# Mixer 0 and the dense experts: w1 loaded, bounded and split at the start of the mixer, and GpSimd's token halves made to wait for the normalised tiles

## What is computed

```python
# mixer of layer 0: a short convolution, linear attention with prefix sums, a gate, then dense experts
y = xp[:, 0:Tv]*w_dw[:,0] + xp[:, 1:Tv+1]*w_dw[:,1] + xp[:, 2:Tv+2]*w_dw[:,2]
x = x + einsum('btd,ed->bte', y, w_pw)
q, k, v = split(einsum('btd,ed->bte', x, w_qkv))      # 16 heads of 8, rotated
q_phi, k_phi = elu(q) + 1, elu(k) + 1
num   = einsum('bthd,bthdm->bthm', q_phi, cumsum(k_phi[..., :, None] * v[..., None, :]))
denom = sum(q_phi * cumsum(k_phi))
attn  = einsum('btd,ed->bte', num / (denom + 1e-6), w_o)
x = x + sigmoid(einsum('btd,ed->bte', x - x_before, w_gate) + b_gate) * attn
h = layernorm(x) * ln_g + ln_b
gw  = softmax(h @ w_moe_gate.T)                       # 4 experts, all used
hid = silu(einsum('btd,efd->btef', h, w1) + b1)       # w1: 4 experts x 512 x 128
s = x + einsum('bte,bted->btd', gw, einsum('btef,edf->bted', hid, w2) + b2)
# ffn of layer 0: 16 experts, top 1 with a capacity of 160 tokens, chosen from the layer's first norm
```

## Time and profile before

| what | us |
|---|---|
| runs shown | 1209.11, 1211.19, 1211.15 (median 1211.15) |
| the profiled execution | 1211.67 |
| its span, first to last instruction | 1209.9 |
| mean granted clock of TensorE | 0.987 of full speed |
| PE busy | 1143.2 (94%) |
| POOL busy | 839.1 (69%) |
| DVE busy | 825.1 (68%) |
| ACT busy | 686.0 (57%) |

### The profile page before, as it was taken

One profiled execution on the slowest core, in us unless ns is written; L12 is line 12 of the kernel. 1 busy time (PEld: TensorE's weight loads), 2 busy tenths in 40 slices (PEclk: granted clock), 3 DMA queues, 4 the chain that ended last, 5 costly groups with the idle time before them and its releaser, 6 DMA issues.

```text
span 1209.9 us, 31474 instructions
## 1 busy us (share of the span) xinstructions
PE 1143.2 (94%) x11948; PEld 755.6 (62%) x11948; DVE 825.1 (68%) x2036; ACT 686.0 (57%) x1375; POOL 839.1 (69%) x1109
## 2 busy tenths in 40 slices
PE   4899689989988999999999999999999999999997
PEld 2354456668755567666766666666676666676665
DVE  3778978813585886686687678668757867866552
ACT  2534254347424566666666656666666665665665
POOL 0778530050625788888798797888879879788895
PEclk9999899999989999999999999999999999999998
DMA  8300020022113401302132030230203204023001
GB/s 314 128 1 1 1 79 2 1 79 79 36 43 71 110 16 32 85 14 46 33 67 46 15 80 7 45 81 19 46 19 80 45 2 89 11 45 72 10 3 37
DMA packets 74891, 60.19 MB, mean 50 GB/s; under 512 B 38962, under 2 KB 69298, under 8 KB 73652
## 3 DMA queue, kind: packets, MB, share of 16 engines
q1 hardware_dynamic: 73716, 56.08, 18.7%
q0 software_dynamic: 1024, 2.09, 0.6%
HBM read 19.76 MB, written 4.72 MB: 20 GB/s over the span
## 4 chain that ended last, share of the span: by engine, by line
PE 67%; ACT 2%; DVE 1%; issue 1%; DVEq 0%
PE S L1962 10%; PE S L1963 10%; PE S L1964 10%; PE A L1952 9%; PE O L1976 6%; PE O L1977 5%; PE O L1974 5%; PE M L1943 3%; PE M L1920 2%; PE M L1922 2%; PE M L1921 2%; PE M L1937 1%; PE M L1930 1%; PE M L1928 1%; PE M L1929 1%
## 5 line engine op out<-in xcount | busy, mean ns | idle before, releaser
L1704 POOL TENSOR_TENSOR plow<-prob 128x512 f16<-128x512 f32 (+3 forms) x640 | 588.8, 931 | 94.4 <-ACT prob L2180 70.6
L2180 ACT ACTIVATE prob<-S,keep_sigma 128x512 f32<-128x512 f32 (+3 forms) x640 | 395.7, 625 | 265.0 <-PE S L1964 262.0
L2281 DVE CUSTOM_DVE_ANT_0 junk<-A,mask_rows,part 128x512 bf16<-128x512 f32 (+3 forms) x384 | 249.0, 649 | 98.3 <-PE A L1952 77.2
L1974 PE MATMUL O<-V,prob 128*128 128x65 f16 x2176 | 232.7, 193 | 0.2 <-POOL plow L1704 0.2
L1976 PE MATMUL O<-V,prob 128*128 128x64 f16 x2176 | 232.6, 195 | 0.0
L1977 PE MATMUL O<-V,plow 128*128 128x65 f16 x2176 | 231.7, 192 | 0.0
L1962 PE MATMUL S<-rows 97*128 97x512 f16 (+3 forms) x640 | 223.3, 349 | 3.7 <-ACT prob L2180 3.4
L1963 PE MATMUL S<-rows 96*128 96x512 f16 (+3 forms) x640 | 222.5, 348 | 0.0
L1952 PE MATMUL A<-rows 96*128 96x512 f16 (+3 forms) x640 | 221.2, 346 | 1.3 <-DVE part L2281 1.0
L1964 PE MATMUL S<-rows 96*128 96x512 f16 (+3 forms) x640 | 220.9, 345 | 0.0
L1974 PEld LDWEIGHTS O<-V,prob 128*128 128x128 bf16 x2176 | 203.0, 97 | 23.6 <-POOL plow L1704 0.3
(11 more groups left out here) (390 smaller groups left out, 1913.5 us busy)
## 6 DMA issues: line engine op xcount, KB each, us to landing
rows<-stage_rows SPq DMA_DIRECT2D x64, 256.0 KB, 3.4
V<-stage_v SPq DMA_DIRECT2D x16, 516.0 KB, 4.6
W<-in_W SPq DMA_DIRECT2D x2, 2048.0 KB, 15.7
shifted<-turned SPq DMA_DIRECT2D x32, 128.0 KB, 2.3
rows<-stage_pos SPq DMA_DIRECT2D x64, 64.0 KB, 3.1
w<-in_w SPq DMA_DIRECT2D x2, 1024.0 KB, 9.0
xe_rows<-zero SPq DMA_DIRECT2D x1, 1280.0 KB, 5.3
ye_rows<-xe SPq DMA_DIRECT2D x5, 256.0 KB, 2.7
```

Of the source, the lines that this page charges most:

```text
L1704: pool.tensor_tensor(plow[:, k % PB, 0:w], full, full.bitcast(BF16).rearrange("p (q e) -> p q e", e=2)[:, :, 1], ALU.subtract).then_inc(s_ ...
L1974: pe.matmul(both, high[:, cs, 1], vh[h][:, j, 0:HS + 1], start=(j == 0 and s == 0), stop=False, skip_group_check=True)
L2180: act.activation(prob[:, k % PB, 0:w], S[k % 2][:, 0:w], ACT.Exp, scale=sigma[:, 2 * p + h:2 * p + h + 1]).then_inc(s_exp, 1)
L2281: dve.tensor_tensor_reduce(junk[:, g % 2, 0:w], A[g % 2][:, 0:w], add, -1.0, before, ALU.add, ALU.min, out).then_inc(s_max, 1)
```

## The change

The loads of w1, ln_g and ln_b are issued right behind the mixer's first weights and have a semaphore of their own (`s_w1`). `bound_parts` stands behind the tap matrices, `bounds_summed` in TensorE's beat -9, and the reciprocals in a function `bound_scales` in VectorE's beat -8. ScalarE makes both `w1_high` and the scaled w1 in beat -8, VectorE makes `w1_low` in beat -4 ahead of the key's phi of chunk 0, and GpSimd the three columns in beat -4. GpSimd has nothing behind its beats. In the next block GpSimd waits for eight normalised tiles before its first split, and clears gwT and zero behind the fourth.

```diff
--- before.py
+++ after.py
@@ -168,7 +168,8 @@
 
 
 
-LATER = ("wg", "rank_order", "ln_g", "ln_b", "w_mg", "w1", "b1", "w2", "b2", "below", "W1", "W2", "be1", "be2")
+FIRST_EXPERTS = ("w1", "ln_g", "ln_b")
+LATER = ("wg", "rank_order", "w_mg", "b1", "w2", "b2", "below", "W1", "W2", "be1", "be2")
 
 
 def mixer0(nc, dram, keep, t0):
@@ -217,7 +218,7 @@
         (DEN,), (U,) = banks("denom", 1), banks("unit", 1)
 
         s_x, s_w, s_v = [sem(f"x_loaded{c}") for c in range(NC)], sem("w0_loaded"), sem("dve_step0")
-        s_later, s_scaled = sem("later_loaded"), sem("w1_scaled")
+        s_later, s_w1 = sem("later_loaded"), sem("w1_loaded")
         s_ln, s_sqrt, s_norm = sem("ln_var0"), sem("ln_sqrt0"), sem("ln_ready0")
         s_xn, s_xna = sem("xn_tiles0"), sem("xn_tiles0_act")
         s_pad, s_unit, s_taps = sem("pads0"), sem("unit_set"), sem("taps_made")
@@ -301,6 +302,9 @@
             for dst, src in ((w_dw, "w_dw"), (w_sq, "w_sq"), (cos, "cos0"), (sin, "sin0"), (b_gate, "b_gate"),
                              (w_vrep, "w_vrep"), (sel, "sel0")):
                 sp.dma_start(dst[:], dram[src]).then_inc(s_w, 16)
+
+            for name in FIRST_EXPERTS:
+                sp.dma_start(t0[name][:], dram[name]).then_inc(s_w1, 16)
 
             for name in ("wq", "wk", "wv", "bq"):
                 sp.dma_start(keep[name][:], dram[name]).then_inc(s_later, 16)
@@ -395,7 +399,7 @@
                     if c > 0:
                         pe.wait_ge(s_rec, c)
                     if c == NC - 1:
-                        pe.wait_ge(s_rd, 4)
+                        pe.wait_ge(s_rd, 3)
                     for i in range(TPC):
                         ins = pe.matmul(DEN[:, i * MH:(i + 1) * MH], zu[:, i * P:(i + 1) * P], sel[:, MD, 0:P:MD],
                                         start=True, stop=True)
@@ -406,7 +410,8 @@
                 pe.wait_ge(s_later, LATER_LOADS)
                 pe.wait_ge(s_rec, NC - 1)
                 for i in range(NT):
-                    pe.matmul(L[:, i * RE:(i + 1) * RE], xnT[:, 2 + i * P:2 + (i + 1) * P], wg[:], start=True, stop=True)
+                    ins = pe.matmul(L[:, i * RE:(i + 1) * RE], xnT[:, 2 + i * P:2 + (i + 1) * P], wg[:], start=True, stop=True)
+                ins.then_inc(s_rl, 1)
 
             def bounds_summed():
 
@@ -439,7 +444,7 @@
                     finish(c - 1, m)
                 if u == UNITS - 4:
                     route_logits()
-                elif u == UNITS - 1:
+                elif u == -SC:
                     bounds_summed()
             at_beats(beat)
             wait_out(pe, ("O", NC - 1))
@@ -515,11 +520,12 @@
                 if going:
                     finish(c - 1, m)
                 if u == UNITS:
-                    act.wait_ge(s_rd, 3)
+                    act.wait_ge(s_rd, 2)
                     act.activation(rexp, rdiff, ACT.Exp).then_inc(s_re, 1)
-                elif u == UNITS + 1:
+                elif u == 1 - SC:
                     act.wait_ge(s_ln, 2)
-                    act.activation(w1_high, w1_all, ACT.Copy, scale=scales[:, 0:1]).then_inc(s_sqrt, 1)
+                    act.activation(w1_high, w1_all, ACT.Copy, scale=scales[:, 0:1])
+                    act.activation(w1_all, w1_all, ACT.Copy, scale=scales[:, 0:1]).then_inc(s_sqrt, 1)
                 elif u == UNITS + 5:
                     act.wait_ge(s_ln, 3)
                     act.activation(std[:, 0:EARLY], vare[:, 0:EARLY], ACT.Sqrt).then_inc(s_sqrt, 1)
@@ -568,14 +574,12 @@
                     weighted(u - 1)
                 if coming:
                     projections(c + 1, m)
+                if u == 5 - SC:
+                    pool.wait_ge(s_ln, 2)
+                    for k, v in ((2, t0["ln_g"]), (3, t0["ln_b"])):
+                        pool.tensor_scalar(scales[:, k:k + 1], v[:], scales[:, 1:2], None, ALU.mult)
+                    pool.tensor_tensor(scales[:, 4:5], tops[:, 0:1], tops[:, 1:2], ALU.mult)
             at_beats(beat)
-            pool.wait_ge(s_sqrt, 2)
-            pool.tensor_scalar(w1_all, w1_all, scales[:, 0:1], None, ALU.mult).then_inc(s_scaled, 1)
-            pool.wait_ge(s_scaled, 1)
-            pool.tensor_tensor(w1_low, w1_all, w1_high, ALU.subtract)
-            for k, v in ((2, t0["ln_g"]), (3, t0["ln_b"])):
-                pool.tensor_scalar(scales[:, k:k + 1], v[:], scales[:, 1:2], None, ALU.mult)
-            pool.tensor_tensor(scales[:, 4:5], tops[:, 0:1], tops[:, 1:2], ALU.mult)
 
         @block.vector
         def _(dve):
@@ -594,6 +598,9 @@
                     for t, k, tab in {2: ((qk, "K", cos), (qk2, "KS", sin)), 4: ((qk, "Q", cos),), 5: ((qk2, "QS", sin),)}[m]:
                         wait_sum(dve, (k, c))
                         out((k, c), dve.tensor_tensor(t[:, j, :], bank((k, c))[:], tab[:, span(c)], ALU.mult))
+                if m == 5 and c == 0:
+                    dve.wait_ge(s_sqrt, 2)
+                    dve.tensor_tensor(w1_low, w1_all, w1_high, ALU.subtract)
                 if m in (5, 8):
                     j = KEY if m == 5 else QUERY
                     dve.wait_ge(s_exp, 2 * c + j + 1)
@@ -642,6 +649,22 @@
                 dve.wait_ge(s_last, max(1, u - 1))
                 dve.tensor_tensor_scan(cum[:, u % 3, :], U[:, 0:1].to_broadcast([P, CW]), src, last[:, m:m + 1], ALU.mult,
                                        ALU.add).then_inc(s_cum, 1)
+
+            def bound_parts():
+
+                dve.wait_ge(s_w1, 16 * len(FIRST_EXPERTS))
+                dve.tensor_reduce(parts[:, 0:1], w1_all, AX_X, ALU.max, apply_absolute_value=True)
+                step(dve.tensor_scalar(tops[:, 0:1], t0["ln_g"][:], X_NORM, None, ALU.mult))
+                dve.scalar_tensor_tensor(tops[:, 0:1], t0["ln_g"][:], -X_NORM, tops[:, 0:1], ALU.mult, ALU.max)
+                step(dve.scalar_tensor_tensor(tops[:, 1:2], t0["ln_b"][:], -1.0, t0["ln_b"][:], ALU.mult, ALU.max))
+                step(dve.tensor_tensor(parts[:, 1:2], tops[:, 0:1], tops[:, 1:2], ALU.add))
+                dve.tensor_scalar(parts[:, 0:2], parts[:, 0:2], H_UNIT, None, ALU.mult).then_inc(s_rd, 1)
+
+            def bound_scales():
+
+                dve.wait_ge(s_rl, 1)
+                step(dve.tensor_scalar(tops[:, 0:2], BOUND, 1e-30, None, ALU.max))
+                dve.reciprocal(scales[:, 0:2], tops[:, 0:2]).then_inc(s_ln, 1)
 
             dve.memset(U[:, 0:1], 1.0).then_inc(s_unit, 1)
             dve.memset(last[:], 0.0).then_inc(s_last, 1)
@@ -670,31 +693,20 @@
             dve.wait_ge(s_taps, 2)
             dve.tensor_scalar(taps[0], w_sq[:, 0, :], w_dw[:, 0:1], None, ALU.mult).then_inc(s_taps, 1)
             dve.wait_ge(s_unit, 1)
+            bound_parts()
 
             def bc(t, n):
                 return t.unsqueeze(2).to_broadcast([P, NT, n])
 
-            def bound_parts():
-
+            def route_top():
+
+                logits = L.rearrange("p (n e) -> p n e", e=RE)
+                dve.wait_ge(s_rl, 2)
                 dve.wait_ge(s_later, LATER_LOADS)
-                dve.tensor_reduce(parts[:, 0:1], w1_all, AX_X, ALU.max, apply_absolute_value=True)
-                step(dve.tensor_scalar(tops[:, 0:1], t0["ln_g"][:], X_NORM, None, ALU.mult))
-                dve.scalar_tensor_tensor(tops[:, 0:1], t0["ln_g"][:], -X_NORM, tops[:, 0:1], ALU.mult, ALU.max)
-                step(dve.scalar_tensor_tensor(tops[:, 1:2], t0["ln_b"][:], -1.0, t0["ln_b"][:], ALU.mult, ALU.max))
-                step(dve.tensor_tensor(parts[:, 1:2], tops[:, 0:1], tops[:, 1:2], ALU.add))
-                dve.tensor_scalar(parts[:, 0:2], parts[:, 0:2], H_UNIT, None, ALU.mult).then_inc(s_rd, 1)
-
-            def route_top():
-
-                logits = L.rearrange("p (n e) -> p n e", e=RE)
-                dve.wait_ge(s_rl, 1)
-                dve.wait_ge(s_later, LATER_LOADS)
-                dve.tensor_scalar(tops[:, 0:2], BOUND, 1e-30, None, ALU.max).then_inc(s_rd, 1)
                 step(dve.tensor_reduce(rmax, logits, AX_X, ALU.max))
                 dve.tensor_tensor(rdiff, logits, bc(rmax, RE), ALU.subtract).then_inc(s_rd, 1)
                 dve.tensor_tensor(cand, logits, bc(rmax, RE), ALU.is_ge).then_inc(s_rd, 1)
-                dve.reciprocal(scales[:, 0:2], tops[:, 0:2]).then_inc(s_ln, 1)
-                dve.wait_ge(s_rd, 4)
+                dve.wait_ge(s_rd, 3)
                 step(dve.tensor_tensor(cand, cand, rank_order[:].unsqueeze(1).to_broadcast([P, NT, RE]), ALU.mult))
                 step(dve.tensor_reduce(cmax, cand, AX_X, ALU.max))
                 step(dve.tensor_tensor(onehot, cand, bc(cmax, RE), ALU.is_equal))
@@ -749,8 +761,8 @@
                     product(v)
                 if 0 <= u < UNITS:
                     prefix(u)
-                if u == UNITS - 2:
-                    bound_parts()
+                if u == 1 - SC:
+                    bound_scales()
                 if going:
                     finish(c - 1, m)
                 if coming:
@@ -905,14 +917,14 @@
 
         @block.gpsimd
```

(6 more changed lines are left out.)

## The result

The changed kernel takes 1203.19 us (median of 4 runs, 1201.43 to 1204.56), the kernel before 1210.88 beside it; the ratio is 0.9939, with a 95% interval of 0.9921 to 0.9956. That is 7.7 us less, of 11.6 forecast. In a later comparison with the kernel before it took 1201.34 against 1211.19: ratio 0.9917 (0.9902 to 0.9931). The profiled execution took 1204.56 us.

What follows compares the result with a forecast made beforehand. It took the first mixer's tail to be held by VectorE's casts waiting for GpSimd, and the rest by TensorE. Tail -11.0, start +0.3 and next block -0.9 summed to -11.6, for a median of 1199.6 us, range 1196.0 to 1203.5.

Steps and rivals of the forecast that it cites:

- (a): Mixer's tail: bounds leave VectorE and TensorE there; denominators start 0.7 us earlier, the inversion behind them 0.8.
- (c): Mixer's tail: TensorE's clock stays at full speed; 0.6 us off up to VectorE's product, 1.2 behind it.
- (b): Mixer's tail: without GpSimd's two passes the casts fall from 8.80 us to 2 x 0.2, so -8.4.
- the casts: Sign in the mixer's tail: casts L707 and L709 take about 0.2 us each.
- TensorE's idle time and clock ahead of the projection: Sign in the mixer's tail: TensorE idle about 1 us there, with a granted clock of 1.00.
- the eight tiles: Sign in the next block: the eight normalised tiles take 2.2 us, not 4.92.
- Step (d): Kernel's start: w1, ln_g and ln_b loaded ahead of wq, bounds made there; cost +0.3 us, from +0.1 to +1.1.
- Rival (4): Start: ln_b lands past 40 us, delaying the first products; +17.7 where +0.3 stands, 1217.0; chance 0.03.
- Rival (2): Tail and start: clock does not come back and the start costs 1.1 us; -9.1, 1202.0; chance 0.14.
- Step (e): Mixer's start: VectorE's w1_low subtraction and GpSimd's query sum exclude each other but stay inside 4.2 us of cover; cost 0.
- Step (f): Next block: GpSimd waits for eight normalised tiles; first dense matmuls 0.9 us earlier, from 0 to -1.1.
- the neighbour (3): Dense stage's begin: its first dozen matmuls spared the half-rate clock, another 2 us, 1197.5; chance 0.09.

Runs made afterwards that it cites:

- experiment 1: Kernel before the change, with GpSimd's two passes over w1 left out; ratio to the kernel before 0.9879.
- experiment 12: The changed kernel run again with no edit, beside the kernel before; 1201.34 against 1211.19, ratio 0.9917.
- experiment 6: Changed kernel with the loads of ln_g and ln_b issued ahead of w1; ratio to the kernel before 0.9923.
- 3: Changed kernel with GpSimd's wait for eight normalised tiles undone, gwT and zero cleared behind the first chunk again; ratio to the kernel before 0.9913.
- 11: Changed kernel with only the 16 route logits sent four tiles at a time in beats 30 to 33; ratio to the kernel before 0.9945.
- experiment 5: Changed kernel with three unread 512-column matmuls on TensorE ahead of its wait for the bounds; ratio to the kernel before 0.9928.
- 7: Changed kernel with ln_g and ln_b issued right behind x, ahead of the first weights; ratio to the kernel before 0.9915.
- experiment 9: Changed kernel with VectorE waiting for w1 alone before the maximum, for ln_g and ln_b behind it; ratio to the kernel before 0.9918.
- 2: Changed kernel with bounds taken from data landed by 16 us instead of w1, ln_g and ln_b; ratio to the kernel before 0.9888.
- 4: Changed kernel with the bounds, scales and w1 passes put in the middle of the mixer; ratio to the kernel before 0.9944.

## Why the prediction was right, and where it was off

**The main mechanism, (a) to (c), was right.** The casts waited for GpSimd (experiment 1). Where the clock holds, product to block is 21.55 us in five profiles: -11.2 for the -11.0 of the sum. By its parts, from experiment 12: the last attention product stands 98.48 us behind the query's phi and not 108.00, so -9.5 for the -9.2 of (a) and (b), and from it to the block it is 7.07 us and not 8.72, so -1.7 for the -1.8 of (c). VectorE and TensorE came out together at the block's end, as worked out. In the profiled execution 1.7 us were lost to a fall of the clock behind the logits: 21.55 became 23.25. I had priced the clock only at the place where the kernel before lost it. The time lies 4.5 us above the sum's by the profiled spans: 3.4 at the start, 1.2 and 1.5 in the mixer's middle and tail, less 1.6 behind them. It is inside the stated range of 1196.0 to 1203.5 by 0.3 us only, and that is in part luck: the start missed its own range, +0.1 to +1.1, by 2.6 us, and what came better elsewhere covered some of it. Of the signs that I had set, the casts, TensorE's idle time and clock ahead of the projection, and the eight tiles came as said. The Relu (34.24 for 30.5), the query's phi (41.79 for 37.84) and the next stage (150.18 for 143.9) did not, and the first product, at 30.40, came past the 28 us that I had named as a sign of being wrong.

**Step (d) was mis-sized: "ln_b lands at 22.3 (21.8 to 22.9)", and so "+0.3 with the handovers, from +0.1 to +1.1".** Measured: ln_b landed at 24.4, and taps to phi grew by 3.7. From the list of DMAs after, time from issue to landing:

```profile
ln_g<-in_ln_g SPq DMA_DIRECT2D x1, 0.5 KB, 12.0
ln_b<-in_ln_b SPq DMA_DIRECT2D x1, 0.5 KB, 13.4
```

Issued at 10.31 and 11.01, they land at 22.3 and 24.4; w1 itself landed at 21.4, near the 21.8 of the sum (19.27 and 2.5). I had put five narrow loads at 0.2 us each, by taking what was left between 19.27 and 25.5 after 2.1 MB at 412 GB/s. The two took 0.9 and 2.1. An average over a mixed queue was a bad measure for the landing of one load, and the upper bound built on it was no bound. Behind the landing followed what I had not priced: a small step of 1.00 us (L659) beside GpSimd's product, TensorE without work for 2.59 us, and its clock. (In experiment 12 that step took 0.15 us, and taps to phi was 22.46 all the same.) The cover of 7.23 us that I had seen on VectorE was real, but the bound was TensorE's: its first sums ended at 25.85, and as the bounds took 3.9 us from the landing on, every microsecond of landing past about 22 was paid (an estimate, 25.85 - 3.9). Rival (4) named this place, but worked it out only for a landing past 40 us; its 34.4 us is where the whole gain would be gone, and between that and 22.9 the text had no price. Rival (2) came near the time, with 1202.0, but not by its mechanism: the clock did come back ahead of the projection.

**What lay under the cover did.** ScalarE's two passes took 2.00 and 1.99 us. The subtraction took 2.34 (2.3 by the row taken). Step (e)'s exclusion is in the timeline: the subtraction from 34.70 to 37.04, and GpSimd's sum, 1.27 us alone, takes 3.23 us from 34.93 and ends at 38.16, ahead of ScalarE's Relu at 39.19. So on ScalarE's path the cost was 0. By that rule of the Trainium skill (SBUF — State Buffer, Who interferes with whom) just this was to be seen; the trace agrees, 3.23 for 1.27 us.

On TensorE's path the 0 is not safe. In the changed kernel's first profile and in experiment 6 GpSimd's sum started beside the subtraction and was not done when VectorE came to the key's phi. That phi took 1.75 us in both, where it takes 0.69 undisturbed, and TensorE stood 2.77 and 2.82 us for what VectorE makes of it. In experiments 3, 11 and 12 GpSimd's sum started just behind the phi, which took 0.69, and TensorE stood 1.7 to 1.9 us. The fall of the clock at 38 to 44 us, worth 1.1 us, came in the first two and not in these three. But experiment 5 has 1.65 and 2.85 us there and no fall; so the longer wait alone does not bring it.

**Step (f)** was worth 1.0 us, for 0.9 (9.59 against 10.60). The rest of the gain there is the neighbour (3), the clock at the dense stage's begin, 1.2 us for the 2 of the text; I had given it 0.09 and left it out of the sum.

The gain was carried to the end: from the read of the sent tokens to the second layer's first load it is 86.47 us before and 86.46 after.

## What stays open

Whether one piece of narrow matmuls lets the clock fall. It fell there in 5 of the 11 profiles with the logits in one piece (changed, 1, 5, 7, 9; not in the kernel before, 2, 3, 4, 6, 12) and in 0 of 3 with spread logits. If 5 in 11 is the share anywhere, three without a fall come by chance in one of six ((6/11)^3). The experiments do not settle it.

Open too is what makes the stretch with the routed experts 20 us longer in experiments 1 to 11, and why experiment 1's ratio is better than its stages.

## What to carry to other kernels

When work goes to where an engine is idle, the question is not how long that engine is idle but when the engine behind it asks; subtract the work from that time and see whether the last load lands by then. Wait for each operand where it is read, not for a group of loads ahead of the first use: splitting one wait in two gave back 3.4 us of the start here (in the stage; the ratios are too coarse to show it). And a cast or a tile product whose length is that of a neighbour's instruction is a wait, and goes when the neighbour's work does.

## What the runs showed of the hardware

Two loads of 128 rows of 4 bytes landed 0.9 and 3.0 us behind a load of 1 MB, which itself landed 1.9 us behind the load ahead of it. Loads of one queue did not land in the order of issue: in experiment 9 w1, issued at 9.21, landed at 22.7, and ln_g, issued at 9.90, at 21.5. Behind a wait of TensorE of 2.6 us the granted clock was 0.51 for 3 us, which cost 1.2 us, and three matmuls that nobody reads spared it. The same program had two falls of the clock more in one execution (38 to 44 us and 132 us) than in another, 2.8 us in sum, so one profile of a kernel is not enough to price such a stretch; its nine runs spread from 1198.8 to 1204.6 us.
